# One block sum in four scaled on ScalarE and added on GpSimd in the batches of a gated cross-attention and attention kernel

## The reference

```
h  = layernorm(x)                                  # per token
hq = fp8_quant_dequant(h,   blocks of 1 x 128)
cq = fp8_quant_dequant(ctx, blocks of 128 x 128)   # ctx is used as a weight
x  = x + tanh(g_xattn) * hq @ cq.T
y  = causal_attention(layernorm(x) @ Wb) @ Wp      # 16 heads of 32, fp32
out = x + tanh(g_ffn) * y
```

## Time and profile before

| what | value |
|---|---|
| median of 3 runs | 501.77 us (500.73 to 505.46) |
| profiled execution, its own time | 500.87 us |
| its span | 499.1 us |
| PE busy / DVE busy | 443.6 / 333.3 us |
| ACT busy / POOL busy | 257.2 / 156.5 us |

### The profile page before, as it was taken

How to read it: one execution, slowest core, us unless ns; L and a number is a source line. 1 busy time by engine, 2 the same in 40 slices (tenths; PEclk the granted TensorE clock), 3 DMA queues, 4 the chain that set the end, 5 groups by cost and what they waited for, 6 DMA issues and landing times.

```text
span 499.1 us, 8044 instructions
## 1 busy us (share of the span) xinstructions
PE 443.6 (89%) x2600; PEld 317.4 (64%) x2600; DVE 333.3 (67%) x1093; ACT 257.2 (52%) x510; POOL 156.5 (31%) x282
## 2 busy tenths in 40 slices
PE   0468799998869999999769999999879999999996
PEld 0244577775536788776535788777545778676765
DVE  3899536879993254788997243788997236566733
ACT  1777446567445570558445463448655424363530
POOL 4988775343223300243213400144122100111110
PEclk9989999999979999999988999999998999999999
DMA  6412083324400345324410234514300144234112
GB/s 215 175 33 85 14 260 91 90 71 107 133 1 2 81 105 153 101 53 98 115 61 2 53 95 98 177 39 105 92 23 1 45 104 102 56 94 102 53 44 85
DMA packets 28217, 42.62 MB, mean 85 GB/s; under 512 B 8304, under 2 KB 8688, under 8 KB 28176
## 3 DMA queue, kind: packets, MB, share of 16 engines
q1 hardware_dynamic: 26752, 41.19, 29.7%
q10 hardware_dynamic: 1232, 0.54, 0.5%
q0 software_dynamic: 192, 0.39, 0.3%
HBM read 12.59 MB, written 4.19 MB: 34 GB/s over the span
## 4 chain that ended last, share of the span: by engine, by line
PE 69%; DVE 16%; POOL 5%; ACT 3%; issue 3%; DMA 2%; SPq 0%; POOLq 0%; DVEq 0%; ACTq 0%
PE pv_bank L788 14%; PE mm_bank L613 9%; PE mm_bank L614 8%; PE mm_bank L615 8%; DVE x_all L1261 6%; PE max_bank L757 6%; PE exp_bank L774 6%; DVE max_bank L1293 3%; PE mm_bank L815 2%; PE mm_bank L817 2%; PE mm_bank L816 2%; PE turn_bank L629 2%; PE pv_bank L797 2%; ACT work L1036 2%; DMA ctx_raw<-in_ctx 2%
## 5 line engine op out<-in xcount | busy, mean ns | idle before, releaser
L1293 DVE CUSTOM_DVE_ANT_0 max_bank<-max_bank,causal 128x512 f32<-128x512 f32 (+3 forms) x256 | 121.6, 509 | 58.1 <-PE max_bank L757 49.8
L1036 ACT ACTIVATE work<-exp_bank 128x512 f32<-128x512 f32 (+1 forms) x192 | 94.6, 528 | 89.9 <-PE exp_bank L774 88.8
L527 POOL TENSOR_SCALAR_AFFINE_SELECT work<-work 128x384 f32<-128x384 f32 x64 | 33.5, 524 | 280.6 <-ACT work L1036 280.6
L788 PE MATMUL pv_bank<-work,v_aug 128*33 128x256 f32 (+3 forms) x512 | 78.5, 449 | 0.8 <-POOL work L530 0.8
L757 PE MATMUL max_bank<-k_stack,q_stack 96*128 96x512 f32 x248 | 67.8, 338 | 5.4 <-DVE row_max L1293 5.4
L774 PE MATMUL exp_bank<-q_stack,k_stack 97*128 97x512 f32 (+3 forms) x256 | 69.1, 335 | 3.5 <-ACT work L1036 1.8
L1261 DVE SCALAR_TENSOR_TENSOR x_all<-mm_bank,coef,x_all 128x128 f32<-128x128 f32 x224 | 61.1, 341 | 0.2 <-issue 0.2
L788 PEld LDWEIGHTS pv_bank<-work,v_aug 128*33 128x33 f32 x512 | 28.4, 113 | 49.4 <-issue 40.0
L613 PE MATMUL mm_bank<-xt_hi,w_hi 128*128 128x512 f32 x128 | 54.1, 422 | 1.5 <-POOL w_lo L543 1.5
L774 PEld LDWEIGHTS exp_bank<-q_stack,k_stack 97*128 97x128 f32 x256 | 45.5, 189 | 14.9 <-ACT work L1036 4.8
L1276 DVE SCALAR_TENSOR_TENSOR qk_lo<-mm_bank,col_root,qk_hi 128x512 fp32r<-128x512 f32 x32 | 24.0, 748 | 44.8 <-ACT qk_hi L1007 44.8
(11 more groups left out here) (176 smaller groups left out, 810.8 us busy)
## 6 DMA issues: line engine op xcount, KB each, us to landing
q_stack<-qk_hi SPq DMA_DIRECT2D x128, 64.0 KB, 2.0
k_stack<-qk_hi SPq DMA_DIRECT2D x120, 64.0 KB, 2.0
ctx_raw<-in_ctx SPq DMA_DIRECT2D x16, 256.0 KB, 3.3
x_all<-in_x SPq DMA_DIRECT2D x16, 256.0 KB, 4.6
q_stack<-qk_lo SPq DMA_DIRECT2D x64, 64.0 KB, 2.0
out<-x_all SPq DMA_DIRECT2D x16, 256.0 KB, 2.5
k_stack<-qk_lo SPq DMA_DIRECT2D x60, 64.0 KB, 2.0
work<-in_L_ffn_Wa SPq DMA_DIRECT2D x3, 768.0 KB, 9.4
```

What stands on the lines that cost most here:

```text
L527: pool.affine_select(out=three, in_=three, compare_op=ALU.is_ge, fill=0.0, base=0, pattern=[[0, 3], [1, P]], channel_multiplier=-1)
L788: last = pe.matmul(pv_bank[64 * j:64 * j + D + 1, P * m:T], v_aug[:, m, 2 * u + j, :], prob[j][:, PROB_COL[m]:PROB_COL[m] + T - P * m], st ...
L1036: act.activation(prob[j][:, UNIT_COL[k]:UNIT_COL[k] + UNIT_LEN[k]], exp_bank[(3 * j + k) % 2][:, 0:UNIT_LEN[k]], ACT.Exp, scale=SCALE).the ...
L1293: last = dve.tensor_tensor_reduce(max_bank[unit % 2][:, col:col + width], max_bank[unit % 2][:, col:col + width], causal[:, T - width:T], ...
```

## The change

In the batches too, the block sums with k = 3 (S3, S7, S11, S15 of each of the three prepared batches) leave DVE. ACT gets the entries `s0` to `s3` (`last_product`, four instructions each) and POOL the entries `a0` to `a3` (`add_product`, one instruction each). The counts behind `s_summed` shrink from 16 to 12 a batch, PE's wait for a bank after such a sum goes to `s_fmul` in place of `s_summed`, and the statistics `b` wait for POOL's addition (`s_fadd`). All order strings are written anew.

```diff
 PE_STEPS = [   # steps 0 to 7
-    "W0 rowmax max0 max1 Q2.0 v3.0 max2 v3.12 exp0 max3 exp1 Q2.1 exp2 max4 exp3 max5 Q2.2 exp4 exp5 v3.3",
-    "Q2.3 max0 rowmax max1 W1 pv max2 max3 exp0 K2.0 exp1 W2 max4 exp2 exp3 K2.1 exp4 max5 back exp5 K2.2",
-    "W3 max0 rowmax K2.3 max1 pv Q3.01 back exp0 exp1 Q3.2 max2 Q3.3 max3 exp2 exp3 K3.01 max4 exp4 K3.23 exp5 max5 X0",
-    "max0 max1 rowmax S0 S1 pv max2 max3 S2 X1 exp0 S3 exp1 max4 exp2 S4 X2 max5 exp3 back S5 S6 exp4 exp5",
-    "max0 rowmax S7 S8 max1 pv max2 S9 exp0 exp1 back exp2 max3 exp3 max4 exp4 X3 max5 exp5",
-    "S10 rowmax max0 max1 S11 pv exp0 max2 exp1 S12 max3 exp2 S13 H0 S14 exp3 S15 back max4 exp4 exp5 max5",
-    "max0 max1 rowmax A0 H1 pv exp0 exp1 H2 max2 exp2 max3 exp3 max4 exp4 max5 exp5 back",
-    "H3 rowmax A1 pv q0.0 exp0 exp1 q0.123 k0.0 exp2 k0.12 exp3 back k0.3 q1.0 exp4 q1.1 exp5 q1.2",
+    "rowmax W0 max0 max1 v3.01 max2 v3.2 Q2.0 exp0 v3.3 exp1 max3 Q2.1 exp2 exp3 Q2.2 exp4 max4 max5 exp5 Q2.3 W1",
+    "max0 rowmax pv max1 K2.0 exp0 max2 exp1 K2.1 W2 exp2 max3 back max4 exp3 K2.2 max5 W3 exp4 exp5",
+    "max0 K2.3 rowmax max1 Q3.0 pv exp0 Q3.12 max2 exp1 Q3.3 max3 exp2 exp3 K3.0 max4 exp4 K3.123 max5 exp5 back X0",
+    "S0 max0 max1 S1 rowmax pv S2 max2 S3 max3 X1 exp0 max4 S4 exp1 X2 S5 max5 exp2 S6 exp3 exp4 back exp5",
+    "max0 rowmax S7 S8 max1 pv exp0 max2 S9 exp1 max3 exp2 S10 exp3 max4 back exp4 max5 exp5 X3 S11",
+    "max0 rowmax max1 pv max2 max3 S12 exp0 max4 exp1 H0 max5 S13 exp2 S14 exp3 S15 exp4 exp5 back",
+    "A0 max0 max1 rowmax H1 pv exp0 exp1 H2 exp2 max2 max3 exp3 exp4 max4 max5 exp5 back",
+    "A1 rowmax H3 pv exp0 exp1 q0.01 back q0.23 exp2 k0.01 exp3 k0.2 exp4 exp5 k0.3 q1",
 ]
 ACT_STEPS = [
...
-    "neg K2 copy exp0 exp1 W3 Q3 exp2 C0 exp3 exp4 K3 exp5 X0",
-    "C1 neg C2 X1 copy exp0 exp1 C3 exp2 exp3 exp4 exp5",
-    "X2 neg exp0 copy exp1 exp2 exp3 exp4 exp5",
-    "neg X3 exp0 copy N0 exp1 exp2 exp3 H0 exp4 exp5 N1",
-    "neg H1 N2 N3 exp0 exp1 H2 exp2 exp3 copy exp4 exp5 H3",
-    "neg exp0 exp1 q0 copy exp2 exp3 k0 exp4 exp5 q1",
+    "neg copy exp0 exp1 exp2 exp3 Q3 W3 C0 K3 exp4 X0 exp5",
+    "C1 neg C2 s0 X1 exp0 exp1 copy exp2 X2 exp3 exp4 exp5",
+    "neg s1 C3 exp0 exp1 copy exp2 exp3 exp4 exp5",
+    "X3 s2 neg N0 copy N1 exp0 exp1 exp2 H0 exp3 s3 exp4 exp5 H1",
+    "neg N2 exp0 exp1 H2 exp2 exp3 copy exp4 exp5",
+    "N3 neg H3 exp0 copy exp1 exp2 q0 exp3 k0 exp4 exp5 q1",
 ]
 DVE_STEPS = [
-    "max0 max1 max2 max3 x0 max4 x1 max5",
-    "x2 max0 x3 max1 Q2 max2 L0 m0 max3 L1 max4 max5 L2 norm",
-    "m1 m2 max0 e0 max1 K2 L3 m3 e1 max2 norm max3 max4 Q3 max5 K3",
-    "max0 max1 S0 S1 max2 max3 S2 max4 S3 S4 max5 S5 S6 norm",
-    "max0 S7 max1 b0 max2 S8 b1 max3 norm max4 max5 S9",
-    "S10 S11 max0 max1 t0 b2 max2 t1 S12 t2 S13 max3 S14 t3 H0 max4 max5 S15 norm b3 A0",
-    "max0 max1 H1 max2 max3 H2 max4 max5 norm A1",
-    "H3 q0 norm k0 q1",
+    "max0 max1 max2 max3 x0 x1 x2 max4 max5 Q2",
+    "x3 max0 L0 max1 max2 max3 L1 max4 max5 norm",
+    "m0 max0 m1 L2 K2 e0 max1 m2 L3 max2 m3 max3 e1 Q3 max4 max5 norm K3",
+    "max0 S0 S1 max1 max2 S2 max3 max4 S4 max5 S5 S6 norm",
+    "S8 max0 max1 b0 max2 S9 max3 max4 norm max5",
+    "b1 max0 max1 S10 max2 max3 S12 max4 S13 max5 t0 S14 t1 t2 t3 b2 H0 norm",
+    "A0 b3 H1 max0 max1 max2 max3 H2 max4 max5 norm A1 H3 q0",
+    "k0 norm q1",
 ]
 POOL_STEPS = [
     "zero0 zero1 i0",
-    "zero0 zero1 u0",
-    "u1 zero0 zero1",
-    "u2 u3 zero0 zero1",
     "zero0 zero1",
-    "r0 zero0 zero1 r1",
+    "u0 zero0 u1 u2 zero1 u3",
     "zero0 zero1",
-    "g0 g1 zero0 zero1 g2 g3",
+    "a0 a1 zero0 zero1",
+    "r0 a2 zero0 a3 zero1 r1",
+    "zero0 zero1",
+    "g0 g1 g2 zero0 zero1 g3",
 ]
...
-ACT_FIRST = ("d0 C0 a0 a1 C1 C2 C3 b0 C4 C5 f4 b1 C6 f5 s0 a2 f6 s1 C7 e3 b2 f7 a3 N0 "
+ACT_FIRST = ("d0 C0 C1 a0 C2 C3 a1 b0 C4 C5 f4 C6 b1 f5 a2 s0 f6 a3 s1 b2 C7 f7 e3 N0 "
...
-DVE_FIRST = ("t0 t1 t2 t3 w0 A0 A1 x0 x1 x2 x3 T0 L0 L1 F0 F1 G0 L2 L3 F2 f0 F3 f1 f2 "
+DVE_FIRST = ("t0 t1 t2 t3 A0 A1 w0 x0 x1 x2 x3 T0 f0 L0 L1 F0 L2 F1 f1 G0 L3 f2 F2 F3 "
...
+            def add_product(n, i):
+
+                pool.wait_ge(s_fmul, NT * n + i + 1)
+                pool.wait_ge(s_summed, 12 * n + 3 * i + 3)
+                pool.tensor_tensor(x_tile(n, i), x_tile(n, i), tile_buf[:, i, :], ALU.add).then_inc(s_fadd, 1)
...
                 elif kind == "S":
-                    pe.wait_ge(s_summed, 16 * n - NT + i + 1)
+                    if i % NK == NK - 1:
+                        pe.wait_ge(s_fmul, NT * n + i // NK + 1)
+                    else:
+                        pe.wait_ge(s_summed, 12 * n + 3 * (i // NK) + i % NK + 1)
...
-            def first_product(i):
-                act.wait_ge(s_coef, 1)
-                act.wait_ge(s_turn, i + 1)
-                act.wait_ge(s_cross, NK * i + NK)
+            def last_product(n, i, first=False):
+                act.wait_ge(s_coef, 1 if first else 2 * n + i // 2)
+                act.wait_ge(s_turn, i + 1 if first else 12 * n + NT + i + 1)
+                act.wait_ge(s_cross, 16 * n + NK * i + NK)
...
             def x1_stat(n, i):
 
-                if n == 0:
-                    dve.wait_ge(s_fadd, i + 1)
-                else:
-                    dve.wait_ge(s_summed, 16 * n - NT + NK * i + NK)
+                dve.wait_ge(s_fadd, NT * n + i + 1)
```

More of the change, by code:

```diff
@@ L107 @@
     "max0 max1 max2 max3 max4 max5",
[7 rows of a table removed]
-]
-PE_FIRST = ("f0 w0 w1 f1 w2 f2 f3 w3 w4 f4 w5 S0 S1 f5 S2 S3 f6 S4 w6 S5 S6 S7 w7 S8 "
-     "S9 S10 S11 w8 f7 S12 w9 f8 S13 w10 S14 f9 w11 S15 v0 v1.01 f10 v1.2 f11 v1.3 q0.0 B0 q0.123 k0.0 "
-     "B1 k0.123 V2 M0 M1 q1.01 M2 q1.23 k1.01 M3 k1.2 M4 k1.3 M5")
-ACT_FIRST = ("d0 C0 a0 a1 C1 C2 C3 b0 C4 C5 f4 b1 C6 f5 s0 a2 f6 s1 C7 e3 b2 f7 a3 N0 "
-     "s2 N1 f8 f9 s3 b3 v0 N2 N3 f10 f11 v1 q0 p0 k0 c0 V2 D0 D1 q1 c1 c2 k1 c3")
-DVE_FIRST = ("t0 t1 t2 t3 w0 A0 A1 x0 x1 x2 x3 T0 L0 L1 F0 F1 G0 L2 L3 F2 f0 F3 f1 f2 "
-     "G1 T1 T2 c0 f3 T3 S0 S1 S2 S4 S5 S6 b0 S8 b1 S9 S10 S12 S13 h0 S14 u0 b2 b3 "
-     "h1 u1 u2 u3 h2 h3 B0 B1 q0 k0 M0 M1 M2 M3 q1 M4 M5 k1")
@@ L128 @@
-POOL_FIRST = ("s0 s1 i0 l0 s2 s3 s4 s5 s6 s7 j0 l1 j1 a0 l2 a1 r0 r1 l3 a2 j2 a3 r2 r3 "
-     "o0 j3 g0 g1 D0 g2 g3 D1 p0 v0")
-PE_END = ("q1.3 k1.0 pv k1.12 V0.0 k1.3 back V0.12 max0 max1 V0.3 y0 V1.01 max2 max3 V1.2 y1 V1.3 V2 max4 y2 max5 y3 O0 "
-     "O1 O2 O3")
-ACT_END = "copy c0 k1 V0 y0 c1 y1 c2 V1 V2 y2 y3 c3"
-DVE_END = "k1 norm max0 max1 y0 y1 max2 max3 max4 max5 y2 O0 y3 O1 O2 O3"
[6 rows of a table added]
+    "norm",
+]
+PE_FIRST = ("w0 f0 f1 w1 f2 w2 f3 w3 f4 w4 w5 S0 f5 S1 S2 S3 S4 w6 S5 f6 S6 S7 w7 S8 "
+     "w8 S9 S10 f7 w9 S11 S12 w10 S13 S14 w11 f8 f9 S15 v0 v1.01 f10 f11 v1.23 q0.01 B0 q0.23 B1 k0 "
+     "V2 M0 M1 q1 k1.01 M2 M3 k1.2 M4 k1.3 M5")
@@ new lines @@
+ACT_FIRST = ("d0 C0 C1 a0 C2 C3 a1 b0 C4 C5 f4 C6 b1 f5 a2 s0 f6 a3 s1 b2 C7 f7 e3 N0 "
+     "N1 f8 s2 b3 s3 f9 v0 N2 N3 f10 f11 q0 v1 k0 c0 p0 V2 c1 D0 D1 q1 c2 k1 c3")
+DVE_FIRST = ("t0 t1 t2 t3 A0 A1 w0 x0 x1 x2 x3 T0 f0 L0 L1 F0 L2 F1 f1 G0 L3 f2 F2 F3 "
+     "G1 T1 f3 T2 c0 S0 S1 S2 S4 S5 S6 b0 S8 S9 S10 b1 T3 S12 u0 S13 h0 S14 b2 h1 "
+     "u1 b3 u2 h2 h3 u3 B0 B1 q0 k0 M0 M1 M2 M3 q1 M4 M5 k1")
+POOL_FIRST = ("s0 s1 i0 s2 s3 l0 s4 s5 s6 s7 l1 j0 j1 a0 l2 a1 l3 r0 r1 j2 a2 a3 r2 r3 "
+     "o0 j3 g0 g1 D0 g2 g3 D1 v0 p0")
@@ L138 @@
+PE_END = "k1.0 pv V0.0 k1.12 back k1.3 max0 V0.1 max1 V0.23 V1.0 y0 V1.12 max2 y1 V1.3 max3 max4 V2 max5 y2 y3 O0 O1 O2 O3"
+ACT_END = "copy k1 c0 c1 y0 V0 V1 y1 c2 V2 y2 c3 y3"
+DVE_END = "max0 k1 norm max1 max2 y0 max3 max4 y1 max5 O0 y2 y3 O1 O2 O3"
 END_LAST = {
-    "PE": "Z2 pv Z3 back Z4 Z5 z3 Z6 Z7 Z8 Z9 Z10 Z11",
+    "PE": "pv Z3 back Z4 Z5 z3 Z6 Z7 Z8 Z9 Z10 Z11",
     "ACT": "copy z3",
-    "DVE": "Z2 norm Z3 z3 Z8 Z9 Z10 Z11",
+    "DVE": "Z1 z2 Z2 norm Z3 z3 Z8 Z9 Z10 Z11",
 }
 BEFORE = {
[1 row of a table removed]
[1 row of a table added]
@@ L169 @@
 DVE_CHAIN, POOL_CHAIN = 24, 13
-NEXT_BATCH, NEXT_CONTEXT = set("WXHSqkLNCxmebiur"), set("Acgt")
+NEXT_BATCH, NEXT_CONTEXT = set("WXHSqkLNCxmebiursa"), set("Acgt")
 def parts_of(names, more, ctx_more, late=False):
@@ L568, in _ @@
                 elif kind == "a":
-                    pool.wait_ge(s_fmul, i + 1)
-                    pool.wait_ge(s_summed, 3 * i + 3)
-                    pool.tensor_tensor(x_tile(0, i), x_tile(0, i), tile_buf[:, i, :], ALU.add).then_inc(s_fadd, 1)
+                    add_product(0, i)
                 elif kind == "r":
@@ L597, in body @@
                             scale_up(n, NT + i)
+                        elif kind == "a":
+                            add_product(n, i)
                         elif kind == "r":
@@ L1044, in first_hi @@
                                ACT.Copy).then_inc(s_thi, 1)
-            def first_product(i):
-                act.wait_ge(s_coef, 1)
-                act.wait_ge(s_turn, i + 1)
-                act.wait_ge(s_cross, NK * i + NK)
```

(12 more changed lines are left out.)

## The result

The changed kernel takes 494.77 us (median of 4 runs, 492.80 to 495.12) against 501.25 us (4 runs, 499.19 to 505.46): a recorded ratio of 0.9858, 95% interval 0.9822 to 0.9894, 7.1 us. By the two medians alone it is 6.5 us (0.9871). Ratios here compare fast runs with fast runs. By the profiled executions it is 5.75 us of own time (500.87 to 495.12) and 5.7 us of span (499.1 to 493.4). The forecast was 12.5. The time lies in the range, near its upper end, and in the band of the rival "waits take half of it", not in the forecast's own.

A forecast was written before the change was run, and what follows sets the result against it. DVE was taken to bound three sags (steps 3 to 5 of batches 0 to 2, PE starved), PE most of the rest. 500.87 less 12.5 for the sums, other terms 0, gave 488.4, stated as 488.5 us; range 479 to 496.

The forecast's parts named there:

- waits take half of it: Rival, chance 0.18: DVE idles a tenth of the sag waiting for PE's banks; 496.7 us, or 492 with b3, A0 moved.
- DVE is the bound: Steps 3 to 5 of batches 0 to 2: DVE idles only 0.5 to 1.3 us of 34.4 to 34.8.
- all four are read inside the sag, where DVE never idles, so this is path and not filler: Steps 3 to 5: four sums leaving DVE save 4.2 us per sag, three times, 12.5 us.
- ACT's four scalings at 0: ACT's added 4.6 us a sag fits its idle time: cost 0, up to 1.1 us a batch if exponentials come late.
- POOL's adds at 0: Four adds, 5.1 us a sag, run beside ACT's work: cost 0, up to 1.3 us a batch.
- The rival in which they hold DVE: Rival, chance 0.04: POOL's 12 adds each hold DVE for 1.285 us, 15.4 us back, 503.8 us.
- The longer way to the statistics, PE's wait for a bank: Statistics b wait for PE, ACT and POOL; PE's bank wait goes to ACT: both 0, the latter 1.1 us if late.
- The new orders at 0: Moved entries in all steps: plus 0 to 1.3, minus 0 to 3.4 us, set against each other at 0.
- the seam: End of step 2: ACT does X0 before exp5, so zero1 and the product with V come up to 1.4 us later.
- The clock: Rival, chance 0.22: shorter sags keep PE from dropping to 1.2 GHz; 481 us, down to 477.
- Prologue and last batch at 0: Prologue: reordered DVE list, -1.5 to +1.5 us, taken as 0; last batch: PE full both ways, 0.
- it changes nothing: Rival, chance 0.09: the relay PE, ACT, POOL, DVE is late at every fourth sum; 499 us, within 1%.

The follow-up runs named there:

- c: Against the changed kernel: norm ahead of t1 to t3, b2, H0; A0 behind step 6's product; ACT's H1 behind neg; a3 behind zero1. 502.57 us, 1.0017.

## Why the prediction was right in direction and half wrong in size

1. *"DVE is the bound" and "all four are read inside the sag, where DVE never idles, so this is path and not filler"*: this is the step that failed. The sags did become shorter by 3.46 to 3.65 us, near the 4.2, but with the offload alone, the very thing that the 4.2 was worked out for, by 0.75, 1.04 and -0.38. A busy share of 98% says that the stretch can't be shorter than DVE's work. It does not say that it gets shorter with it: ACT's list in step 3 (0.64 us of it shown by moving C3) and the relay over exp0, `copy` and `back` in step 4 were nearly as long. Of DVE's work, 33.78 us in the first sag became 30.17, 3.6 less: the four sums are 4.2 (17.5 to 13.3), but one more unit of row maxima (0.7) and the first two instructions of A0 (0.5) now fall between the two products.
2. *ACT's four scalings at 0, up to 1.1 in step 3*: the bound was right and the choice wrong for the old order (step 3 longer by 0.7 us), right for the new one, where C3 has left: ACT 8.21 of 10.21 us.
3. *POOL's adds at 0*: held. 1.276 us each for the expected 1.285; nobody waits for them but the statistics, 0.3 us in the whole run. The rival in which they hold DVE did not come: sums at 344 ns, statistics at 686 for 684. But `u`, POOL's scaling to the fp8 range, which the prediction put at 0 in its new place in step 2, does hold DVE: 1.2 us a batch in three small instructions (last section). That this lengthened step 2 is not shown; DVE has 11.36 us of work in its 12.47, less than the nearly 14 of the forecast.
4. *The longer way to the statistics, PE's wait for a bank*: 0 in the change, as forecast; PE's waits for sums went from 1.6 to 0.6 us. In c, where the product was brought forward, the way over a3 and b3 to N2 became the last one, with a wait of 2.61 us.
5. *The new orders at 0*: here the forecast erred most in size, +5 us outside the sags. Step 1 is +1.05 us in each batch, because Q3.0 (0.64 us) and one unit of maxima (0.36) now lie ahead of the next cut: work moved that I had put down as "a stretch of the same kind, at 0". That would be neutral if step 2 shrank by as much; it gave 0.10 of it back, and the seam, priced at 0 to 1.4, took the rest. Moving b3 and A0 to step 6 was to be worth 0 to 1.3 us a batch in a hole of DVE. They did not reach the hole: b3 starts 0.23 us ahead of the product with V of step 6 and was 0.70 ahead of it before, and in both kernels DVE goes on from there with H1 and maxima and idles only after them. Step 6 is longer by 0.29, 1.31 and 0.43. Steps 5 and 6 together are -0.59, +0.54 and -0.67. The hole is still there, 2.65 us for `max_bank` where it was 2.53 in the earlier trace rows, which I read as made by PE, at half clock there, and not by a lack of DVE work.
6. *The clock*: it falls as before, to 0.51 at 140 to 144 us, and the product after it takes 3.79 us for 3.86. The argument against this rival held: PE idles in step 5 just as it did.
7. *Prologue and last batch at 0*: -0.3 us, within the bounds, and +0.5 us, for which no bounds were given.

By terms: forecast -12.5 in the sags and 0 outside; measured -10.7 and +5.0. The rival "waits take half of it" had the time right, but not the mechanism: DVE idles 0.66 us of 30.83 in the sag, not a tenth. The loss is in the steps around it. So the direction and the range came true, but not by the forecast's sum: the sags gave nearly what it said only because offload and new orders came together, and the loss around them was still covered by the width of the range. Two slips bear on nothing above: the terms of the rival "it changes nothing" give 499.7 us, not 499, and DVE does other instructions than sums, maxima and statistics in steps 4 and 5 too (`norm` and H0).

## What to carry to other kernels

A busy share near 100% tells the most that an offload can bring, the work moved, and not that it will bring it. Before costing it as pure gain, list for each step the second longest chain (here ACT's list, and PE waiting for ACT's copy), because it is what remains. Here offload and new order are one change: alone they measured +0.2% and +0.6%, together -1.4%, so trying one at a time would have thrown both away. And when a chain is taken out and a step stays long, look at who is full then: in step 4 it was DVE again, partly by an entry (b1) that could wait. Last, cut both traces at the same recurring instruction before explaining a difference; the cut shows which gain is returned, and where.
